# Scores negated and scaled in the masked pass, two norms applied by ScalarE, three unread products ahead of the first loads

## What is computed

```python
x = _layernorm(x + attn(x))        # 16 heads, 4 key heads, D = 128, window W = 128
x = _layernorm(x + xattn(x, ctx))  # x @ softmax(query(ctx) @ key(ctx).T).T
x = _layernorm(x + moe(x))         # 2 shared and 16 routed experts, 4 chosen, FF = 176

# inside attn, for each block of 128 tokens and each head
scores = einsum('bnqhd,bnkhd->bnhqk', qb, kw) * scale        # scale = 1/sqrt(128)
scores = where(mask, scores, -1e30)
probs = softmax(scores, axis=-1)
# layer norm
(x - mean(x)) / sqrt(var(x) + 1e-5)
```

## Time and profile before

| what | us |
|---|---|
| runs: median (lowest, highest) | 426.19 (423.72, 426.29) |
| the profiled execution, its own time | 425.41 |
| its span, first to last instruction | 423.6 |
| PE busy | 390.4 (92%) |
| DVE busy | 312.7 (74%) |
| ACT busy | 259.2 (61%) |
| POOL busy | 181.9 (43%) |
| span from 16 to 77 (rest of batch 0's attention) | 61 |
| one batch in the loop (from one second norm to the next) | 60.3 |

### The profile page before, as it was taken

How to read it: one execution, slowest core, us unless ns; L and a number is a source line. 1 busy time by engine, 2 the same in 40 slices (tenths; PEclk the granted TensorE clock), 3 DMA queues, 4 the chain that set the end, 5 groups by cost and what they waited for, 6 DMA issues and landing times.

```text
span 423.6 us, 8510 instructions
## 1 busy us (share of the span) xinstructions
PE 390.4 (92%) x2553; PEld 347.9 (82%) x2553; DVE 312.7 (74%) x868; ACT 259.2 (61%) x653; POOL 181.9 (43%) x314
## 2 busy tenths in 40 slices
PE   3977898999988999998999888999999999999995
PEld 2666687999976998887999777888988998999995
DVE  1595999788898697997897987778767645744445
ACT  3557988677746776655685658465585744443443
POOL 0053557446365545554653654478776500000000
PEclk9996999999999999999999999999999999999998
DMA  7611150100000000000000059432133221342321
GB/s 205 251 50 52 50 175 0 28 2 0 2 2 6 20 0 0 0 0 0 0 0 0 0 143 338 139 105 90 66 97 91 85 79 51 98 142 86 98 68 50
DMA packets 24678, 28.26 MB, mean 67 GB/s; under 512 B 2961, under 2 KB 17194, under 8 KB 24650
## 3 DMA queue, kind: packets, MB, share of 16 engines
q1 hardware_dynamic: 24650, 27.92, 20.8%
HBM read 26.80 MB, written 1.11 MB: 66 GB/s over the span
## 4 chain that ended last, share of the span: by engine, by line
PE 67%; DVE 16%; issue 8%; POOL 3%; ACT 3%; DMA 1%; SPq 1%; DVEq 0%; POOLq 0%; ACTq 0%
PE bank L696 18%; PE bank L697 17%; PE bank L698 17%; PE bank L826 4%; PE bank L835 3%; PE bank L825 2%; PE bank L798 2%; DVE by_cos L1320 2%; DVE pT_lo L1200 1%; DVE by_sin L1321 1%; PE bank L898 1%; DVE scores L1331 1%; PE bank L792 1%; DVE xln L1388 1%; POOL factor L1631 1%
## 5 line engine op out<-in xcount | busy, mean ns | idle before, releaser
L1009 ACT ACTIVATE hid<-bank,b_cols 128x512 f32<-128x512 f32 x48 | 33.0, 688 | 61.0 <-PE bank L698 50.1
L1217 DVE TENSOR_TENSOR hid<-hid,gate_rows 128x512 f32<-128x512 f32 (+1 forms) x44 | 32.4, 737 | 43.4 <-ACT hid L1009 43.1
L1590 POOL TENSOR_SCALAR nprobs<-probs,rsums 128x128 f32<-128x128 f32 x64 | 24.2, 378 | 88.6 <-DVE rsums L1338 80.0
L697 PE MATMUL bank<-w_lo,hid_hi 128*128 128x256 f32 (+1 forms) x200 | 56.3, 282 | 0.0
L1582 POOL TENSOR_TENSOR queryT<-by_cos,by_sin 128x512 f32<-128x512 f32 x32 | 42.5, 1330 | 28.7 <-DVE by_sin L1321 27.7
L1069 ACT COPY swapped<-bank 64x512 f32<-64x512 f32 x40 | 23.3, 583 | 32.8 <-PE bank L698 32.6
L1200 DVE TENSOR_TENSOR hid_lo<-hid,hid_hi 128x512 fp32r<-128x512 f32 x48 | 36.2, 753 | 5.4 <-ACT hid_hi L1030 5.4
L696 PE MATMUL bank<-xT_hi,wq_hi 128*128 128x256 f32 x128 | 38.4, 300 | 1.8 <-issue 1.2
L698 PE MATMUL bank<-x2T_hi,w_lo 128*128 128x512 f32 (+1 forms) x100 | 39.6, 396 | 0.0
L697 PEld LDWEIGHTS bank<-w_lo,hid_hi 128*128 128x128 f32 (+1 forms) x200 | 37.6, 188 | 2.1
L1076 ACT ACTIVATE probs<-scores,ntop 128x128 f32<-128x128 f32 x64 | 25.8, 403 | 21.1 <-DVE ntop L1334 20.5
(11 more groups left out here) (174 smaller groups left out, 1265.5 us busy)
## 6 DMA issues: line engine op xcount, KB each, us to landing
gate_rows<-gates_d SPq DMA_DIRECT2D x16, 256.0 KB, 3.1
stage<-in_L_attn_q_kernel SPq DMA_DIRECT2D x4, 512.0 KB, 6.6
stage<-in_L_attn_out_kernel SPq DMA_DIRECT2D x4, 512.0 KB, 3.6
w_raw<-in_L_ffn_routed_w SPq DMA_DIRECT2D x2, 1024.0 KB, 10.1
gate_rows<-gates_d SPq DMA_DIRECT2D x8, 224.0 KB, 2.9
gate_rows<-gates_d SPq DMA_DIRECT2D x8, 192.0 KB, 2.8
gate_rows<-gates_d SPq DMA_DIRECT2D x8, 160.0 KB, 2.4
w_raw<-in_L_ffn_routed_w SPq DMA_DIRECT2D x2, 528.0 KB, 7.1
```

Of the source, the lines that this page charges most:

```text
L697: nc.tensor.matmul(o, sh, ml, start=False, stop=False, **kw)
L1009: nc.scalar.activation(hid[:, u % 2, :], z_bank[u % 3][:], ACT.Relu, bias=b1_cols[:, i % NC:i % NC + 1]).then_inc(relu_done, 1)
L1217: nc.vector.tensor_tensor(own, own, gate_rows[rows, i % 3, :], ALU.mult).then_inc(gated, 1)
L1590: nc.gpsimd.tensor_scalar(nprobs[:, u, 0:W], probs[:, u, 0:W], rsums[:, u, 0:1], 1.0, ALU.mult, ALU.mult)
```

## The change

Three things are changed.

First, mask_and_top hands minus the scale to the fused instruction and takes the minimum in place of the maximum, so that `scores` holds the negated, scaled scores and `ntop` comes straight out of the accumulator. The exponential then has the scale -1. The instruction L1334 and its semaphore are gone; ACT waits on score_read.

Second, `normed` moves from DVE to ACT, as Identity with a scale and a bias per partition. The bias (minus the mean times the inverse root) is carried through the Newton steps as a third row of `newton`, which is why DVE makes one more small instruction (`negated[:, 1, :]`) and POOL's products are over 4 and 6 numbers where they were over 2 and 4. The places in the order are new: 25.2 and 28.95 on ACT, for 24.25 and 27.5 on DVE.

Third, DVE sets 512 columns of `nprobs` to one at its very start, and PE multiplies them with themselves into bank 2: twice ahead of its wait for ident, once more between the transposes of x and the wait for the context. Nobody reads the results.

```diff
-            "residual": 22.75, "moments 1": 23, "moments 2": 26.75, "normed 1": 24.25,
-            "normed 2": 27.5},
+            "residual": 22.75, "moments 1": 23, "moments 2": 26.75},
+    "act": {"slot": 0, "exp": 0.75, "probs_hi": 3, "heads_hi0": 7.25, "heads_hi1": 9.25,
+            "normed 1": 25.2, "normed 2": 28.95},
...
+            def keep_busy(n):
+
+                for _ in range(n):
+                    nc.tensor.matmul(bank[2][:], idle_rows[:, 0:P], idle_rows[:, 0:HALF], start=True, stop=True)
...
                 if work == "ctx turned":
 
+                    keep_busy(1)
                     e.wait_ge(ld_ctx, 16 * 5)
...
+            e.wait_ge(idle_set, 1)
+            keep_busy(2)
             e.wait_ge(ld_ident, 16)
...
-                e.wait_ge(top_done, head_count(b, h))
+                e.wait_ge(score_read, head_count(b, h))
...
-                                     scale=SCALE, accum_out=psums[:, w, 0:1])
+                                     scale=-1.0, accum_out=psums[:, w, 0:1])
...
+            def normed(b, which):
+
+                m = 2 * b + which
+                e.wait_ge(newton_done, NEWTON_STEPS * (m + 1))
+                e.sem_inc(act_passed, 1)
+                for t in range(TT):
+                    ins = nc.scalar.activation(xln[:, t, :], xln[:, t, :], ACT.Identity, bias=newton[:, 2, t:t + 1],
+                                               scale=newton[:, 0, t:t + 1])
+                ins.then_inc(ln_done, 1)
...
+                if i == 4:
+                    normed(z, 0)
+                if i == 9:
+                    normed(z, 1)
...
-                nc.vector.tensor_tensor_reduce(scores[:, u, W:3 * W], o[:, W:3 * W], mask[:], 1.0, NEVER,
-                                               ALU.add, ALU.max, top[:, u, 1:2]).then_inc(score_read, 1)
-                e.wait_ge(score_read, head_count(b, h))
-                nc.vector.tensor_scalar(ntop[:, u, :], top[:, u, :], -SCALE, None, ALU.mult).then_inc(top_done, 1)
+                nc.vector.tensor_tensor_reduce(scores[:, u, W:3 * W], o[:, W:3 * W], mask[:], -SCALE, FAR,
+                                               ALU.add, ALU.min, ntop[:, u, 1:2]).then_inc(score_read, 1)
...
+                nc.vector.tensor_scalar(negated[:, 1, :], moments[:, :, 0:1].rearrange("p t a -> p (t a)"), -1.0, None, ALU.mult)
...
+            nc.vector.memset(idle_rows[:, 0:HALF], 1.0).then_inc(idle_set, 1)
...
-                settled(nc.gpsimd.tensor_tensor(yv, y, half_neg[:], ALU.mult))
+                settled(nc.gpsimd.tensor_tensor(newton[:, 1:3, :], negated[:], by_root(y, 2), ALU.mult))
...
+                    settled(nc.gpsimd.tensor_tensor(newton[:], newton[:], by_root(factor[:], 3), ALU.mult))
```

More of the change, by code:

```diff
@@ L60 @@
 NEVER = -3e38
+FAR = 3e38
 I32 = mybir.dt.int32
@@ L331, in decoder_layer @@
         var_eps = sb("var_eps", [P, TT])
-        half_neg = sb("half_neg", [P, TT])
-        newton = sb("newton", [P, 2, TT])
+        negated = sb("negated", [P, 2, TT])
+        newton = sb("newton", [P, 3, TT])
         factor = sb("factor", [P, TT])
@@ L555, in decoder_layer @@
         E_BANK = [6, 7, 4, 5]
+        idle_rows = nprobs[:].rearrange("p a k -> p (a k)")
         block = es.enter_context(nc.Block())
@@ L1328, in mask_and_top @@
                 o = score_bank[u]
-                nc.vector.tensor_tensor_reduce(scores[:, u, 0:W], o[:, 0:W], mask[:, W:2 * W], 1.0, NEVER,
-                                               ALU.add, ALU.max, top[:, u, 0:1])
-                nc.vector.tensor_tensor_reduce(scores[:, u, W:3 * W], o[:, W:3 * W], mask[:], 1.0, NEVER,
-                                               ALU.add, ALU.max, top[:, u, 1:2]).then_inc(score_read, 1)
-                e.wait_ge(score_read, head_count(b, h))
-                nc.vector.tensor_scalar(ntop[:, u, :], top[:, u, :], -SCALE, None, ALU.mult).then_inc(top_done, 1)
+                nc.vector.tensor_tensor_reduce(scores[:, u, 0:W], o[:, 0:W], mask[:, W:2 * W], -SCALE, FAR,
+                                               ALU.add, ALU.min, ntop[:, u, 0:1])
+                nc.vector.tensor_tensor_reduce(scores[:, u, W:3 * W], o[:, W:3 * W], mask[:], -SCALE, FAR,
+                                               ALU.add, ALU.min, ntop[:, u, 1:2]).then_inc(score_read, 1)
             def recip(b, h):
@@ L1379, in moments_of @@
                 nc.vector.tensor_scalar(var_eps[:], var, EPS, 1.0, ALU.add, ALU.mult)
-                nc.vector.tensor_scalar(half_neg[:], var, EPS, -0.5, ALU.add, ALU.mult).then_inc(moments_done, 1)
-            def normed(b, which):
-                m = 2 * b + which
-                e.wait_ge(newton_done, NEWTON_STEPS * (m + 1))
-                e.sem_inc(dve_passed, 1)
-                for t in range(TT):
-                    ins = nc.vector.tensor_scalar(xln[:, t, :], xln[:, t, :], moments[:, t, 0:1],
-                                                  newton[:, 0, t:t + 1], ALU.subtract, ALU.mult)
-                ins.then_inc(ln_done, 1)
+                nc.vector.tensor_scalar(negated[:, 1, :], moments[:, :, 0:1].rearrange("p t a -> p (t a)"), -1.0, None, ALU.mult)
+                nc.vector.tensor_scalar(negated[:, 0, :], var, EPS, -0.5, ALU.add, ALU.mult).then_inc(moments_done, 1)
             n = [0]
@@ L1433, in once @@
                     step(ins, work)
-            for s in (score_read, top_done, rsum_done, pT_done):
+            for s in (score_read, rsum_done, pT_done):
                 e.sem_inc(s, AHEAD)
```

25 lines of the change are left out of this document (9 added, 16 removed).

## The result

On one chip, in turns with the kernel before, the changed kernel takes 410.51 us (409.84 to 410.99) and the kernel before 424.96 (422.83 to 426.29). The ratio is 0.966, with an interval of 0.961 to 0.971: 14.45 us less. The forecast was 415.5 with a range from 411.5 to 420.5. The direction and the places came out as forecast, the size did not: 10.5 us were summed up and 14.45 came, and 410.51 lies outside the range. Of the 5.0 us between 415.5 and 410.51, about 1 is no part of the sum: the forecast was taken from a median of 426.19 for the kernel before, and a fourth run, of 422.83, brought that to 424.96.

What follows compares the result with a forecast made beforehand. PE was taken to set the pace in the loop and DVE in the first batch. Terms 2.8 + 0.1 + 1.2 + 5.5 + 0.9 = 10.5 us took the profiled 425.41 to 414.9; forecast 415.5, range 411.5 to 420.5.

Steps and rivals of the forecast that it cites:

- The start: First 16 us: ones products raise PE's clock early, so q0 starts 2.8 us earlier (bounds 1.2 and 3.2).
- the late rise: At the start: PE's clock might rise only at 8.3 us instead of 6.3; 0.2 us taken off for it.
- The rival that the ones do nothing: At the start: clock rises late anyway or weights' arrival takes over; 2.8 us less gain, 418.3; chance 0.12.
- The clock's fall: Near 36 us: half clock after PE's pauses costs 2.2 us; kept in the sum at its old cost.
- the rival with 0.17: Near 36 us: the clock's fall goes too, 2.2 us more gained, 413.2 us; chance 0.17.
- passes on to the end: Stage behind the start, up to 30 us, waits for q0, so the whole 2.8 us gain reaches the end.
- ntop in the first batch: 43 to 77 us: removing 11 ntops frees 3.5 us of DVE; a third comes through, 1.2 us (0.5 to 2.5).
- The first head: At 28.67 us: the wait for POOL's queryT moves from ntop to e_exp; gain 0.1 us (0 to 0.7).
- The rival that ends slower: Masked pass: minimum costs more than maximum, outweighing the gain from 0.66 us a head; 434 at 1 us; chance 0.03.
- The norms in the loop: Three loop batches: 1.3 us at the first norm and 0.55 at the second per batch, 5.5 us in all.
- The rival that ACT is no better placed than DVE: Loop norms come late behind ACT's own queue; 5.5 us becomes 2.1, giving 418.9; chance 0.13.
- Batch 3: Pause of 0.57 at its first expert norm goes; with the locked ntop at 260, 0.9 us (-0.5 to 1.0).

Runs made afterwards that it cites:

- e1: The kernel before with only the three products on ones and their memset added: 422.03 us, ratio 0.9933.
- e4: The changed kernel without the products on ones: 414.10 us, ratio 0.9762 to the kernel before.
- e8: The changed kernel itself, unchanged, run and profiled again: 411.61 us, ratio 0.9700 to the kernel before.
- e7: The changed kernel with one unread 512-column product on PE ahead of its wait for e_norm in each of the last two turns: 410.71 us.
- e2: The kernel before with only the minimum form of the masked pass, and so without ntop: 419.34 us, ratio 0.9859.
- e5: The changed kernel with an unread 128x2 tensor_scalar on DVE behind every masked pass, the exponential not waiting for it: 414.52 us.
- e9: The changed kernel with a 128x2 reciprocal on DVE behind every masked pass, the exponential waiting for it: 414.46 us.
- e3: The kernel before with only the two norms moved from DVE to ACT: 417.64 us, ratio 0.9833.

## Why the prediction was right and wrong

**The start: 3.2 us, forecast 2.8.** In the changed kernel's timeline of PE and of its weight loads (the answers to the earlier trace rows; start, length, what ended the pause):

```profile
1.93 3.54 PE L700 MATMUL bank<-nprobs 128*128 128x512 f32 x4 [1.93 <-DVE nprobs L1458]
5.30 0.60 PE L795 MATMUL bank<-ident,xb 128*128 128x128 f32 x4
5.74 1.02 PE L700 MATMUL bank<-nprobs 128*128 128x512 f32 x2
7.64 0.44 PE L896 MATMUL bank<-ident,xw 128*128 128x128 f32 x2 [0.88 <-DMA ctx_sb<-in_ctx]
...
9.82 0.67 PE L907 MATMUL bank<-ctxT,xwT 128*128 128x512 f32 x1 [0.88 <-DVE ctxT L1429]
...
2.94 0.34 PEld L700 LDWEIGHTS bank<-nprobs 128*128 128x128 f32 x1 [0.52 <-issue]
3.80 0.34 PEld L700 LDWEIGHTS bank<-nprobs 128*128 128x128 f32 x1 [0.52 <-issue]
...
10.33 0.19 PEld L907 LDWEIGHTS bank<-ctxT,xwT 128*128 128x128 f32 x1 [0.24 <-issue]
10.76 0.19 PEld L907 LDWEIGHTS bank<-ctxT,xwT 128*128 128x128 f32 x1 [0.24 <-issue]
11.19 0.19 PEld L907 LDWEIGHTS bank<-ctxT,xwT 128*128 128x128 f32 x1 [0.24 <-issue]
```

The first halves follow by 0.86 us, those of L907 by 0.43 from the first pair on: PE is at full clock ahead of the context. The transposes of x and the third product run at it already (the four transposes in 0.60 us), so the clock had risen by 5.3 us; the step said 6.3, at the latest 8.3. The third product is long over when the context lands. So the late rise, for which 0.2 were taken off, didn't happen, and q0 is at 12.93 for a forecast of 13.1 to 13.3. The rival that the ones do nothing is refuted by e1. The steps and the upper bound (3.2) were right. e4 lacks only the ones and is 2.5 us slower than e8 and 3.6 slower than the changed kernel's first median (e4 and e8 are from different chips).

**The clock's fall.** Forecast to stay, since its pauses stay. They are 1.30, 1.65 and 1.90 us in the changed kernel, for 1.63 and 1.84 in the earlier trace rows:

```profile
26.70 1.38 PE L933 MATMUL bank<-ident,e_exp 128*128 128x128 f32 x8 [1.30 <-DVE e_exp L1446]
...
31.82 0.66 PE L933 MATMUL bank<-ident,e_exp 128*128 128x128 f32 x4 [1.65 <-DVE e_exp L1446]
...
34.37 0.66 PE L933 MATMUL bank<-ident,e_exp 128*128 128x128 f32 x4 [1.90 <-DVE e_exp L1446]
```

It stayed, and was 3.4 us long in the one profile and 6.8 in the other (e8). Its going, the rival with 0.17, was right in place and local price (2.2 us, e7), but not in its worth to the end in the changed kernel: 0.9. The step "passes on to the end", right for the start, would have been wrong here: PE meets DVE's splits of the weights and values in the stage behind. In the kernel before it may have been right. Of its executions beside the experiments the five at a mean clock of 1.00 took 423.28 to 423.81 us, the twelve at 0.989 to 0.992 took 424.86 to 426.17. They have no profile, so that difference wasn't followed.

**ntop in the first batch: this is the step that failed.** It read: DVE gives up 3.5 us between 43 and 77, PE has only 3.3 us of pauses there, some behind POOL and ACT, "so a third of that comes through: 1.2 us (0.5 to 2.5)". Measured: 3.73 us, and 3.33 in e8; e2 alone gives 3.72. More came through than PE had pauses. Here are PE's first pause of that stage and its largest, before, and then the busy time from the transposes of cent_sb to those of x of batch 1, before and after (columns as in the earlier trace rows):

```profile
47.16 0.55 PE L835 MATMUL bank<-ident,nprobs 128*128 128x128 f32 x3 [0.53 <-POOL nprobs L1591]
...
71.27 0.52 PE L835 MATMUL bank<-ident,nprobs 128*128 128x128 f32 x3 [0.85 <-DVE pT_lo L1200]
```

```profile
43.97:74.75 30.78, 27.95 (x181) 23.77 (x181) 30.45 (x90) 26.82 (x73) 19.91 (x25) 1.00 0.24 78
```

```profile
39.97:67.01 27.04, 26.95 (x182) 23.82 (x182) 26.57 (x82) 25.98 (x72) 19.49 (x25) 1.00 0.28 88
```

Three things were wrong in the step. The share of a third had no row under it. It set aside the pauses behind POOL, but those, three for nprobs with 1.2 us together, went as well: nprobs waits for the exponential, and that waited for ntop. Second, PE's pauses are no upper bound. They fell from 2.83 to 0.09 us between these two places, and the same products counted 1.0 us less as busy, so PE must have stood inside stretches that the profile counts as busy, too. The time of DVE, which was busy for 30.45 of 30.78 us, was the better measure: ntop held it for 3.9 us between 43 and 77 (3.5 was the mean over the kernel times eleven), and DVE's work from place to place fell by 3.9. Third, ntop was counted as time of DVE alone. It stood between the masked pass and the exponential, so it delayed ACT and POOL behind it as well. e5 and e9 tell the two apart. With an instruction of ntop's form that nobody waits for, 2.07 us come back in this stage, not 1.2 (29.51 us from place to place for 27.44 in e8; e5's profile is of its slowest execution, but its falls of the clock lie ahead of this stage); with a reciprocal in its place in the chain, making the exponential wait for it costs 1.56, six times its cost as bare work (0.25).

**The first head.** Forecast 0.1 (0 to 0.7), since DVE's next large instruction would wait for the same product of POOL. It gave 0.35 at attT 3, inside the bounds, and e2 alone gives the same. The wait did move: the first e_exp starts at 25.56 and its pair takes 1.09 us for 0.62, while queryT runs until 26.23.

**The masked pass** keeps its time: the half of 256 columns is at 419 ns median for the mean of 417 in the earlier trace rows, the other at 280. The line of it in the changed kernel (lowest, median, highest):

```profile
L1357 DVE CUSTOM_DVE_ANT_0 scores<-bank,mask x64: 411/419/423, 25.0 to 244.6; 128x256 f32<-128x256 f32 x64
```

The rival that ends slower, with the minimum dearer by 0.66 us or more per head, falls with it.

**The norms in the loop.** Forecast 1.85 us per batch and 5.5 in all; measured 2.25 per batch. First ACT's instruction, by its line, and then the two places of batch 0, for the earlier trace rows:

```profile
L1098 ACT ACTIVATE xln<-xln,newton x16: 586/596/606, 109.6 to 288.5; 128x256 f32<-128x256 f32 x16
...
109.56 1.10 ACT L1098 ACTIVATE xln<-xln,newton 128x256 f32<-128x256 f32 x2
...
110.71 0.66 PE L800 MATMUL bank<-ident,xln 128*128 128x128 f32 x4 [0.18 <-ACT xln L1098]
...
111.40 0.69 DVE L1327 COPY x1T<-bank 128x512 f32<-128x512 f32 x1 [1.57 <-PE bank L800]
...
112.24 1.12 PE L806 MATMUL bank<-attT,x1T 128*128 x4
...
121.34 0.20 POOL L1646 TENSOR_TENSOR newton<-newton,factor 128x6 f32<-128x6 f32 x1
...
121.51 0.19 ACT L1089 ACTIVATION_READ_ACCUMULATOR probs<-scores,ntop 128x1 f32 x1
121.66 1.10 ACT L1098 ACTIVATE xln<-xln,newton 128x256 f32<-128x256 f32 x2
...
122.81 0.66 PE L800 MATMUL bank<-ident,xln 128*128 128x128 f32 x4 [0.67 <-ACT xln L1098]
```

The pair takes 1.10 us on ACT (forecast 1.05) and nothing of POOL's is waited for. The first norm's pause went from 0.76 to 0.18, by 0.58 (forecast 0.59). DVE stood idle for 1.57 us until the transposes and copied at once; the product with attT has no pause ahead of it, and the lead grows by 0.82 there (forecast 0.71). The second norm's pause went from 1.37 to 0.67, by 0.70, for a forecast of 0.45 of the instruction and 0.55 in all. Together 2.1; the 0.15 that are left to 2.25 were not placed. The same mechanisms, each a little larger than summed: 0.4 a batch and 1.2 us over three, and a further 0.2 in batch 0, where the table has 2.47 from the transposes of x to the second norm. The rival that ACT is no better placed than DVE falls: in e3 alone the norms bring 1.94 a batch, and 6.4 us by the spans.

**Batch 3.** 0.43 at its first norm, where the pause of 0.57 is gone as forecast (ACT's two tiles start at 271.76, PE follows at 273.00 without a pause worth a mark), and 0.47 from there to the end: 0.90 for 0.9.

**The sum.** In the profiles 15.6 came for 10.5: the start 0.4 more, the first head 0.25, the rest of the first batch 2.5, the shorter fall 0.5, the loop 1.4 (they sum to 5.05 for a difference of 5.1). Half of the miss is the one step on ntop. Its upper bound, 2.5, was itself too low by 1.2, and so the range was: with every other term where it came and ntop at its guess the forecast would have been near 413, still 2.5 us too high. The range was also narrower than its terms: their upper bounds (3.2, 0.7, 2.5, 7.5, 1.0) add up to 14.9 us, which is 411.3 and not the 412.5 given for them.

## What to carry to other kernels

Where an engine is busy for 99% of a stage, a small instruction on it is not bounded by the next engine's pauses, or a share of them: here 3.73 us came for 3.31 of pauses. Take the instruction's own time in that stage as the upper estimate (3.9), from its rows there and not from its mean, and follow each pause back to what it waits for, through other engines too. A small instruction costs more for where it stands (between a result and its reader, or beside another engine that holds what its form needs) than for its own length; fold it into its neighbour. Work that nobody reads is worth its place on TensorE while it waits for the first data, but what it gives later in the kernel is only as much as the next stage leaves.

## What the runs showed of the hardware

- A tensor_scalar of 128x2 on DVE, which takes 0.16 us alone, took up to 1.28 us beside POOL's products queryT and keyT and ended with them, in all 15 cases of e5 (87.41 and 87.39 us above); a reciprocal of the same size, at the same distance into such a product, took 0.16, and over 64 of them 0.151 to 0.165. The Trainium skill (SBUF — State Buffer, "Who interferes with whom") says that a tensor_scalar can take VectorE's second pair of ports, which it shares with GpSimd and which one of the two holds for a whole instruction. By that rule the trace agrees for those products and for the reciprocal. It doesn't for nprobs: 11 of e5's tensor_scalars start inside it and none is held (0.156 to 0.166 us); in the kernel before one of four is, at 259.71.
- The granted clock fell while PE had pauses of 1.30, 1.65 and 1.90 us (behind the second of them in e8, behind the third in the changed kernel's first profile), and stayed at its upper level where the last two were cut to 0.79 and 1.06 by a product of 512 columns each (e7).
- With the ones products the start hardly varies: q0 comes between 12.90 and 13.33 us in the ten profiles that have them, and between 15.56 and 17.01 in the four that haven't. The runs spread less too, by 1.1 us between lowest and highest in the changed kernel for 3.5 before, but that isn't shown to be the start's doing: before, the quick executions are those without a fall of the clock, as told above.
- An Identity with scale and bias per partition over 128x256, from SBUF to SBUF on ACT, takes 596 ns, two in a row 1.10 us.
